# Softmax denominators from ones columns beside the values, divided between two 32x32 block transposes

## The chip, the core and the metric

One core of a Trainium2 chip runs the kernel. The metric is the device time of one execution in microseconds (us). Its engines work side by side and are tied by semaphores: TensorE (PE: matmuls, and PEld: the weight loads that go with them), VectorE (DVE), ScalarE (ACT), GpSimd (POOL), and SyncE (SP), which here only issues DMAs.

## The reference, cut to what matters

Input x is 8 images of 64 channels and 32x32 pixels, float32. The first layer is a window transformer block: layer norm over channels, windows of 8x8 = 64 tokens, 8 heads of depth 8, a relative position bias, softmax, projection and residual, a second layer norm, an MLP with gelu and its residual. The second layer is a gated convolution (a pointwise layer, a top-k mask over channels, depthwise 3x3, 5x5 and 7x7 kernels fused with a 1x1 layer). The part that the change touches:

```python
attn = einsum('bnhd,bmhd->bhnm', q * scale, k) + bias
attn = softmax(attn, axis=-1)                  # exp(a - max) / sum over the 64 keys
out = einsum('bhnm,bmhd->bnhd', attn, v).reshape(Bn, N, C)
return out @ w_proj + b_proj
```

## The kernel before, in words

**Layout.** Channels stand on the partitions, two images at once (partition 64*bh + channel), and the 4 x 1024 columns of pixels are cut in NG = 8 groups of G = 512 columns. One group holds NW = 8 windows (times two images). Each engine has its own program, written out by hand, and waits on counting semaphores; the order of the statements in each program is the order of its work.

**The attention phase** (38 to 201 us) is a software pipeline over the groups, `step(g, ...)`, once on each engine (PE L891, ACT L604, DVE L1236, POOL L456). Steps 0 and 1 stand alone, a hardware loop runs steps 2 and 3, then steps 4 to 7 stand alone. Step g of PE holds:
- `scores(g, w)` for w = 0 to 7 (L821): one matmul with the negative maxima (L832) and six with keys and queries split in a high and a low part (L835). ACT takes the exponentials of each window into `probs` (L581). `scores(g, 0)` waits for the maxima (`dv_minus`) and for the key blocks of this group (`k_blocks_in`); the instruction at which these waits are seen is L832.
- `values(g+1)` (L795), which ACT copies into `v_blocks` (`evacuate_v`, L576); `centered(g+2)` and `variance(g+2)` (helper line L763), the layer norm two groups ahead, with POOL making the low part of the squares (L286); `projection(g-1)` (L867), `centered2(g-1)` and `variance2(g-1)` for the second norm (L763 too).
- `weighted_values(g, 0)` and `sums(0)` after `scores(g, 4)`; then the passes over group g+1 that find the row maxima (`scores_for_max`, L813), woven between scores 5, 6 and 7, each reduced by DVE (`take_maximum`, L1189); `keys(g+2)` (L785, waits for maximum 5), `transpose_maxima(g+1)` (L819, waits for maximum 7), `queries(g+2)` (L790), and last `weighted_values(g, 1)` and `sums(1)`.

**The pieces that the change touches.** `weighted_values(g, quad)` (L839) multiplies the unnormalised probabilities of four windows with `v_blocks`: for each window p, each half of heads hh and each head j of the half one matmul of 32 stationary columns and 64 moving ones. In the 32 columns the values of a head fill two blocks of 8 (one for each image) and the rest is zero; hh = 1 accumulates onto hh = 0 in the same place of the PSUM bank PV, columns 0 to 255. `sums(quad)` (L853) runs the probabilities of the four windows against constant ones (L859) to get the denominators, laid out as the numerators are, in columns 256 to 511 of PV. On DVE, `divide_by_sums(g, quad)` (L1201) takes the reciprocal of those 256 columns (L1203) and multiplies (L1205) into `attended`. Quad 0 stands in DVE's step between maximum 2 and maximum 3 of the next group, quad 1 at the end of the step, behind `k_low` (L1179) and `q_low` (L1184). `weighted_values` waits for the `dv_att` of the quad before, because it writes PV again; `projection` waits for `dv_att` of both quads.

**The queue of SP.** In a fixed order, group by group: `spread_key_blocks(g+1)` (L385, four DMAs of 128 KB, after all scores of group g are done: `pe_scores`), `spread_queries(g+1, 1)` (L398, eight DMAs), `spread_keys(g+2)` (L371, eight DMAs), `spread_queries(g+2, 0)` (L398, eight).

**At the start** ACT loads its tables, sets all of `v_blocks` to zero in one operation (L522, waits for `eps_set`), and then waits for the first matmul. DVE copies the first constants (L1113) after the DMA `center_in`.

**After 201 us** come the MLP (L978, L990), the pointwise layer (L1002) and the gates, and from 247 us on the convolution (L1066), where PE is busy nearly throughout. The first of them are `mlp1(0)` and half of `mlp1(1)`, and then `projection(7)`.

## Time and profile before

| | us |
|---|---|
| runs | 345.48, 345.36, 343.74 (median 345.36) |
| the profiled execution, its own time | 343.12 |
| its span, first to last instruction | 341.3 |
| attention phase, first scores to last sums | some 163 of it |
| PE / DVE / ACT / POOL busy | 302.2 / 237.4 / 221.4 / 58.0 |
| TensorE's granted clock, mean | 0.98 of full speed; 1.00 from 38 us on up to the end of the attention |

The profiled execution takes 1.8 us more than its span, and was 0.6 to 2.4 us quicker than the three runs. Busy times of different engines overlap, so no one of them tells what a change is worth; the chain of waits and the timeline of a step do.

### The profile page before, as it was taken

The numbers are of one execution on the slowest core, as the hardware profiler recorded it, in microseconds if no ns is written. First come the engines' busy times: TensorE is split into PE (matmuls) and PEld (weight loads), VectorE is DVE, ScalarE is ACT, GpSimd is POOL, SyncE is SP. The second block draws the span as 40 slices with busy tenths as digits, with TensorE's granted clock in tenths as the row PEclk, the third lists the DMA queues.
The fourth block names the chain that finished last, engine by engine and source line by source line (L and its number), as shares of the span: only waits on it lengthen the run. The fifth ranks groups of instructions, "written<-read, shape, count | busy, mean of one in ns | idle before, by whom it ended". The sixth has DMA issues, their size and how long they took to land.

```text
span 341.3 us, 6607 instructions
## 1 busy us (share of the span) xinstructions
PE 302.2 (89%) x2570; PEld 215.9 (63%) x2570; DVE 237.4 (70%) x411; ACT 221.4 (65%) x371; POOL 58.0 (17%) x56
## 2 busy tenths in 40 slices
PE   2826888999999999999997999699899999999993
PEld 2514675767768776677675864354277777777772
DVE  2997148289496794976959635668999999976311
ACT  7693854867777677776673587986991673754500
POOL 4311001131331313313011160222220000000000
PEclk9987899999999999999999999999999999999999
DMA  7741154123141141411414000077003686777911
GB/s 170 152 92 53 51 144 84 48 50 80 50 83 48 40 95 47 80 48 41 94 52 89 17 2 0 1 162 160 0 3 70 131 181 133 147 139 154 189 32 31
DMA packets 31148, 27.67 MB, mean 81 GB/s; under 512 B 21008, under 2 KB 27664, under 8 KB 31120
## 3 DMA queue, kind: packets, MB, share of 16 engines
q1 hardware_dynamic: 30544, 26.48, 36.1%
q10 hardware_dynamic: 576, 0.79, 1.0%
q8 instruction: 20, 0.33, 0.5%
q14 instruction: 8, 0.07, 0.1%
HBM read 3.78 MB, written 2.10 MB: 17 GB/s over the span
## 4 chain that ended last, share of the span: by engine, by line
PE 58%; ACT 14%; DVE 13%; SPq 5%; DMA 4%; issue 3%; POOL 2%; DVEq 0%; ACTq 0%
PE psum L1066 25%; PE psum L835 5%; DVE maxima L1189 5%; PE psum L990 3%; PE psum L978 3%; PE psum L785 3%; PE psum L813 3%; PE psum L763 3%; ACT v_blocks L576 3%; DVE inv_sum L1203 2%; ACT q_blocks L566 2%; POOL parts L286 2%; ACT probs L581 2%; PE psum L850 2%; DMA probs<-in_raw 2%
## 5 line engine op out<-in xcount | busy, mean ns | idle before, releaser
L1066 PE MATMUL psum<-shifted,conv_w 128*128 128x512 f32 x336 | 86.6, 419 | 0.0
L1066 PEld LDWEIGHTS psum<-shifted,conv_w 128*128 128x128 f32 x336 | 63.9, 191 | 21.6 <-issue 1.3
L835 PEld LDWEIGHTS psum<-q_heads,k_blocks 128*128 128x128 f32 x384 | 54.6, 189 | 5.7 <-issue 1.9
L581 ACT ACTIVATE probs<-psum 128x512 f32<-128x512 f32 x64 | 38.1, 599 | 30.5 <-PE psum L835 30.3
L835 PE MATMUL psum<-q_heads,k_blocks 128*128 128x256 f32 x384 | 56.0, 281 | 0.0
L1189 DVE TENSOR_REDUCE maxima<-psum 128x8 f32<-128x512 f32 x64 | 40.3, 682 | 13.7 <-PE psum L813 12.7
L286 POOL TENSOR_TENSOR parts<-x,parts 128x256 fp32r<-128x256 f32 (+1 forms) x21 | 20.2, 975 | 84.0 <-ACT parts L589 51.1
L763 PE MATMUL psum<-parts,center_average 128*128 128x512 f32 x64 | 23.7, 454 | 11.9 <-DVE parts L286 6.8
L813 PE MATMUL psum<-k_heads,q_blocks 128*128 128x256 f32 x128 | 23.4, 306 | 12.1 <-DVE maxima L1189 5.0
L832 PE MATMUL psum<-minus_max,pick 128*128 128x512 f32 x64 | 30.1, 471 | 1.1 <-ACT probs L581 0.5
L813 PEld LDWEIGHTS psum<-k_heads,q_blocks 128*128 128x128 f32 x128 | 19.3, 201 | 17.7 <-DVE maxima L1189 6.1
L1203 DVE RECIPROCAL inv_sum<-psum 128x256 f32<-128x256 f32 x16 | 28.0, 1748 | 2.9 <-PE psum L859 2.8
L286 POOL TENSOR_TENSOR parts<-square_logvar,parts 128x512 fp32r<-128x512 f32 x14 | 18.2, 1301 | 68.5 <-ACT square_logvar L534 54.3
L272 ACT CAST conv_w<-conv_w 32x896 fp32r<-32x896 f32 x31 | 29.1, 938 | 0.4
L1433 DVE SCALAR_TENSOR_TENSOR x<-psum,weights,x 64x512 f32<-64x512 f32 x16 | 12.0, 748 | 21.0 <-PE psum L1066 20.9
L706 ACT CAST conv_w<-whole_w 128x896 fp32r<-128x896 f32 x8 | 7.5, 937 | 27.5 <-DVE whole_w L1408 18.8
L679 ACT ACTIVATE hidden<-psum,mlp_bias 128x512 f32<-128x512 f32 x32 | 19.6, 700 | 2.6 <-PE psum L978 2.6
L763 PEld LDWEIGHTS psum<-parts,center_average 128*128 128x128 f32 x64 | 10.3, 200 | 15.9 <-POOL parts L286 7.8
L566 ACT CAST q_blocks<-q_parts 32x512 fp32r<-32x512 f32 x32 | 19.7, 616 | 0.6
L978 PE MATMUL psum<-normed,mlp_w 128*128 128x512 f32 x64 | 18.1, 422 | 1.0 <-ACT hidden L679 1.0
L850 PEld LDWEIGHTS psum<-probs,v_blocks 128*32 128x32 f32 x1024 | 15.0, 110 | 6.2 <-issue 5.1
L492 POOL TENSOR_TENSOR images<-square_logvar,images 128x512 fp32r<-128x512 f32 x8 | 10.7, 1338 | 42.1 <-ACT images L689 42.1
(139 smaller groups left out, 463.8 us busy)
## 6 DMA issues: line engine op xcount, KB each, us to landing
shifted<-images SPq DMA_DIRECT2D x32, 332.5 KB, 5.5
k_blocks<-k_parts SPq DMA_DIRECT2D x32, 128.0 KB
q_heads<-q_parts SPq DMA_DIRECT2D x128, 32.0 KB, 1.8
k_heads<-k_parts SPq DMA_DIRECT2D x64, 32.0 KB, 1.8
out<-x SPq DMA_DIRECT2D x8, 256.0 KB, 4.7
x<-in_x SPq DMA_DIRECT2D x6, 256.0 KB, 4.9
x<-in_x SPq DMA_DIRECT2D x4, 128.0 KB, 4.3
weights<-in_weights ACTq DMA_DIRECT2D x1, 443.0 KB, 9.0
```

The costliest lines, as they stand in the source:

```text
L272: ins = copy(conv_w[bh][shift * KS:(shift + 1) * KS, part, :, C:], w[(shift - 1) * KS:shift * KS, :, 0:C])
L286: return engine.tensor_tensor(low, whole, high.bitcast(F32), ALU.subtract)
L566: ins = act.copy(q_blocks[r, half, :, bh * T:(bh + 1) * T].rearrange("p (s w) t -> p s w t", s=2), q_parts[r, par, :, 0, :].bitcast(F32).r ...
L581: act.activation(probs[:, w, :], psum[:, PROB0 + w % 2, :], ACT.Exp).then_inc(S["ac_probs"], 1)
L763: ins = pe.matmul(psum[:, bank, :], center_average[:, which, :], parts[:, part, :], start=part == 0, stop=part == 1)
L813: ins = pe.matmul(max_bank(w)[:, hh * G // 2:(hh + 1) * G // 2], q_blocks[:, hh, w, :], of_half(k_heads, hh)[:, :, w * T:(w + 1) * T], sta ...
L832: pe.matmul(bank, pick[:, w, :], minus_max[:, :, :], start=True, stop=False)
L835: ins = pe.matmul(bank[:, hh * G // 2:(hh + 1) * G // 2], k_blocks[:, hh, w // (NW // 2), k_part, w % (NW // 2), :], of_half(q_heads[:, q_ ...
L978: ins = pe.matmul(psum[:, HIDDEN0 + m, :], mlp1_w[:, part, f * 128:(f + 1) * 128], normed2[:, bh, bass.ds(n * G, G)], start=part == 0, sto ...
L1066: ins = pe.matmul(psum[:, CONV0 + bh, :], conv_w[bh][:, w_part, t, :], img[:, y:y + H - 1:2, x0:x0 + W], start=t == 0 and w_part + part == ...
L1189: dve.tensor_reduce(maxima[:, w * NH:(w + 1) * NH], max_bank(w).rearrange("p (h t) -> p h t", t=T), AX.X, ALU.max).then_inc(S["dv_max"], 1)
L1203: dve.reciprocal(inv_sum[:], psum[:, PV, 256:512]).then_inc(S["dv_inv"], 1)
```

## The change

The zeros beside the values become ones: a constant `sum_columns` (columns 16 to 31 are one where the row's image and the column's block agree) is copied over all of `v_blocks` at the start, after the first constants have landed. A value matmul then gives 16 rows of numerators and 16 of denominators for one half of heads; the two halves go side by side in PV instead of accumulating, so it still has 32 matmuls a quad, and `sums` is gone. Numerators and denominators then lie in different partitions, so DVE transposes the bank in blocks of 32x32 into `by_query`, takes the reciprocal of 32 numbers a partition, multiplies twice (128 numbers a partition each), and transposes the result back into `attended`. PE waits for the first transpose (`dv_turned`) before it writes PV again. Each of DVE's five instructions waits for the one that it reads from.

```diff
@@ -53,12 +53,11 @@
 
     "center": np.where(_bh[:, None] == _bh, (_p[:, None] == _p) - 1.0 / C, 0),
     "average": np.where(_bh[:, None] == _bh, 1.0 / C, 0),
+    "sum_columns": (np.arange(32) >= 16)[None] & (_bh[:, None] == np.arange(32) % 16 // HD),
     "ident": _p[:, None] == _p,
     "reverse": (_p % T)[:, None] == T - 1 - _p % T,
     "head_of_row": (_p % NH)[:, None] == np.arange(NH),
     "window_of_row": C * ((_p // NH % NW)[:, None] == np.arange(NW)),
-    "ones_by_head_half": (np.arange(64) // 32 == np.arange(64) % 32 // 16)[None]
-    & (_bh[:, None] == np.arange(64) % 16 // HD),
     "earlier": np.arange(C) < (_p % KS)[:, None],
     "valid": _valid(),
     "batch_of_row": _p[:, None] == np.arange(B),
@@ -90,7 +89,7 @@
 _RAT, NRAW = _columns(_RAW)
 
 
-NFIRST = _AT["average"][1]
+NFIRST = _AT["sum_columns"][1]
 
 
 def _constants():
@@ -171,8 +170,9 @@
         normed, rstd = (at(n, [128, G]) for n in ("normed", "rstd"))
         attended, rstd2 = (at(n, [128, G]) for n in ("attended", "rstd2"))
         projected = square2
-        inv_sum = at("inv_sum", [128, 4 * T])
+        inv_sum = at("inv_sum", [128, 2 * 4 * T // 32, 2])
         parts = at("parts", [128, 2, G], F32R)
+        by_query = at("by_query", [128, 2 * 4 * T // 32, 4, HD])
 
 
         normed2 = at("normed2", [128, 2, COLS], F32R)
...
@@ -518,9 +518,9 @@
 
             LN_AND_EXP, GELU = 6, 10
             load_tables(LN_AND_EXP)
-            act.wait_ge(S["eps_set"], 1)
-            act.activation(v_blocks[:].rearrange("p a b -> p (a b)"), eps[:, 0:1].to_broadcast([128, 2 * NW * NH * 32]), ACT.Copy, scale=0.0
-                           ).then_inc(S["v_zeroed"], 1)
+            act.wait_ge(S["center_in"], 16)
+            act.activation(v_blocks[:].rearrange("p a (b c) -> p (a b) c", c=32),
+                           const("sum_columns").unsqueeze(1).to_broadcast([128, 2 * NW * NH, 32]), ACT.Copy).then_inc(S["v_set"], 1)
 
             def high_of_x(n):
 
@@ -634,6 +634,7 @@
 
             square_of_centered(0)
             act.dma_start(weights[:, _WAT["vec"][1]:], d["weights"][:, _WAT["vec"][1]:]).then_inc(S["weights_in"], 16)
+            act.wait_ge(S["eps_set"], 1)
             act.wait_ge(S["consts_in"], 16)
             for half in range(2):
                 ins = act.activation(k_blocks[:, half, :, 0], reversal().rearrange("p (s w) t -> p s w t", s=2), ACT.Copy, scale=not_in_half(half))
@@ -645,7 +646,7 @@
             evacuate_k(0, 0)
             evacuate_q(0, 0)
             block_queries(1, 0)
-            act.wait_ge(S["v_zeroed"], 1)
+            act.wait_ge(S["v_set"], 1)
             evacuate_v(0, 0)
             square_of_centered(1)
             late = range(NW // 2, NW)
@@ -841,23 +842,15 @@
                 pe.wait_ge(S["ac_v"], 4 * (g + 1))
                 pe.wait_ge(S["ac_probs"], NW * g + 4 * quad + 4)
                 if not (isinstance(g, int) and g == 0 and quad == 0):
-                    pe.wait_ge(S["dv_att"], 2 * g + quad)
+                    pe.wait_ge(S["dv_turned"], 2 * g + quad)
                 for p in range(4):
                     for hh in range(2):
                         for j in range(4):
                             w, head = 4 * quad + p, 4 * hh + j
-                            at = (w * NH + head) * 32 - 16 * hh
-                            pe.matmul(psum[32 * j:32 * j + 32, PV, p * T:(p + 1) * T], v_blocks[:, par, at:at + 32],
-                                      probs[:, w, head * T:(head + 1) * T], start=hh == 0, stop=hh == 1)
-
-            def sums(quad):
-
-                for hh in range(2):
-                    for j in range(4):
-                        head = 4 * hh + j
-                        a = _AT["ones_by_head_half"][0] + 32 * hh
-                        ins = pe.matmul(psum[32 * j:32 * j + 32, PV, 256:512], consts[:, a:a + 32],
-                                        probs[:, 4 * quad:4 * quad + 4, head * T:(head + 1) * T], start=hh == 0, stop=hh == 1)
+                            at = (w * NH + head) * 32
+                            column = (hh * 4 + p) * T
+                            ins = pe.matmul(psum[32 * j:32 * j + 32, PV, column:column + T], v_blocks[:, par, at:at + 32],
+                                            probs[:, w, head * T:(head + 1) * T], start=True, stop=True)
                 ins.then_inc(S["pe_pv"], 1)
 
             def projection(c):
@@ -908,7 +901,6 @@
                     variance(far)
                 scores(g, 4)
                 weighted_values(g, 0, par)
-                sums(0)
                 maximum_pass(0, 1)
                 scores(g, 5)
                 maximum_pass(2, 3)
@@ -927,7 +919,6 @@
                 if far is not None:
                     queries(far)
                 weighted_values(g, 1, par)
-                sums(1)
 
             pe.wait_ge(S["dv_center"], 1)
             centered(0)
@@ -1110,7 +1101,7 @@
 
             dve.memset(eps[:], EPS1).then_inc(S["eps_set"], 1)
             dve.wait_ge(S["center_in"], 16)
-            dve.tensor_copy(center_average[:].rearrange("p m c -> p (m c)"), consts[:, 0:NFIRST]).then_inc(S["dv_center"], 1)
+            dve.tensor_copy(center_average[:].rearrange("p m c -> p (m c)"), consts[:, 0:_AT["average"][1]]).then_inc(S["dv_center"], 1)
             dve.wait_ge(S["x_first"], 32)
             for s in range(2):
                 ins = dve.tensor_copy(stripe(parts[:, 0, :], s), x_view(0, s))
@@ -1199,11 +1190,24 @@
                                   const("head_of_row").unsqueeze(2).to_broadcast([128, NH, T]), ALU.mult).then_inc(S["dv_minus"], 1)
 
             def divide_by_sums(g, quad):
-                dve.wait_ge(S["pe_pv"], 2 * g + quad + 1)
-                dve.reciprocal(inv_sum[:], psum[:, PV, 256:512]).then_inc(S["dv_inv"], 1)
-                dve.wait_ge(S["dv_inv"], 2 * g + quad + 1)
-                dve.tensor_tensor(attended[:, quad * 4 * T:(quad + 1) * 4 * T], psum[:, PV, 0:4 * T], inv_sum[:],
-                                  ALU.mult).then_inc(S["dv_att"], 1)
+
+                n = 2 * g + quad + 1
+                dve.wait_ge(S["pe_pv"], n)
+                if not (isinstance(n, int) and n == 1):
+                    dve.wait_ge(S["dv_att"], n - 1)
+                dve.transpose(by_query[:].rearrange("p n k d -> p (n k d)"), psum[:, PV, :]).then_inc(S["dv_turned"], 1)
+                dve.wait_ge(S["dv_turned"], n)
+                dve.reciprocal(inv_sum[:], by_query[:, :, 2:4, 0]).then_inc(S["dv_inv"], 1)
+                dve.wait_ge(S["dv_inv"], n)
+                blocks = 4 * T // 32
+                for hh in range(2):
+                    mine = slice(hh * blocks, (hh + 1) * blocks)
+                    ins = dve.tensor_tensor(by_query[:, 0:blocks, 2 * hh:2 * hh + 2, :], by_query[:, mine, 0:2, :],
+                                            inv_sum[:, mine, :].unsqueeze(3).to_broadcast([128, blocks, 2, HD]), ALU.mult)
+                ins.then_inc(S["dv_ratios"], 1)
+                dve.wait_ge(S["dv_ratios"], n)
+                dve.transpose(attended[:, quad * 4 * T:(quad + 1) * 4 * T], by_query[:, 0:blocks].rearrange("p n k d -> p (n k d)")
+                              ).then_inc(S["dv_att"], 1)
 
             def add_residual(c):
                 dve.wait_ge(S["ac_proj"], c + 1)
```

## Rows read from the trace of the kernel before

**Rows 1.** The page, part 4: the chain that ended last, by engine.

```profile
PE 58%; ACT 14%; DVE 13%; SPq 5%; DMA 4%; issue 3%; POOL 2%; DVEq 0%; ACTq 0%
```

**Rows 2.** The chain in order of time, step 3 into step 4: start us, us, what.

```profile
115.24 1.67 DVE inv_sum L1203
116.94 0.42 DVE attended L1205
...
119.30 1.10 PE psum L785 x2
...
121.89 1.03 PE psum L850 x64
122.92 0.86 PE psum L859 x16
123.79 0.43 PE psum L832
...
137.01 1.67 DVE inv_sum L1203
```

**Rows 3.** Groups by line and form: busy us, mean ns of one | idle before.

```profile
L1203 DVE RECIPROCAL inv_sum<-psum 128x256 f32<-128x256 f32 x16 | 28.0, 1748 | 2.9 <-PE psum L859 2.8
L859 PE MATMUL psum<-probs,consts 128*32 128x256 f32 x256 | 16.7, 379 | 0.0
```

**Rows 4.** The same view: the nearest rows to DVE's new operations.

```profile
L1189 DVE TENSOR_REDUCE maxima<-psum 128x8 f32<-128x512 f32 x64 | 40.3, 682 | 13.7 <-PE psum L813 12.7
L1211 DVE TENSOR_TENSOR x<-square_logvar,x 128x256 f32<-128x256 f32 x16 | 6.1, 422 | 14.1 <-ACT square_logvar L585 14.1
L1370 DVE TENSOR_TENSOR gate_memory<-gate_memory 128x128 f32<-128x128 f32 x2 | 0.6, 291 | 0.1
```

**Rows 5.** Timeline, SP's key blocks and PE's first scores after them, steps 0 and 3.

```profile
51.84 2.72 SPq L385 DMA_DIRECT2D k_blocks<-k_parts  x4
58.41 0.50 PE L832 MATMUL psum<-minus_max,pick 128*128 128x512 f32 x1
...
117.73 2.74 SPq L385 DMA_DIRECT2D k_blocks<-k_parts  x4
```

**Rows 6.** The chain in order of time, end of step 5 to step 7.

```profile
174.20 1.79 DMA k_heads<-k_parts
...
181.12 0.61 SPq L385
...
183.13 3.39 DMA k_blocks<-k_parts
...
186.76 0.47 PE psum L832
```

**Rows 7.** Timeline, POOL and DVE reading SBUF: steps 3 and 5.

```profile
116.54 1.29 POOL L286 TENSOR_TENSOR parts<-square_logvar,parts 128x512 fp32r<-128x512 f32 x1 [1.99 <-ACT square_logvar L594]
120.67 1.41 POOL L286 TENSOR_TENSOR parts<-x,parts 128x256 fp32r<-128x256 f32 x2 [2.84 <-ACT parts L528]
121.36 1.26 DVE L1198 TENSOR_TENSOR minus_max<-maxima_t,consts 128x512 fp32r<-128x512 f32 x1
...
164.90 0.69 DVE L1198 TENSOR_TENSOR minus_max<-maxima_t,consts 128x512 fp32r<-128x512 f32 x1
```

**Rows 8.** Timeline, step 7 and behind it: start us, us, what [idle before].

```profile
193.82 1.28 POOL L286 TENSOR_TENSOR parts<-x,parts 128x512 fp32r<-128x512 f32 x1 [12.61 <-ACT parts L589]
195.48 0.64 PE L763 MATMUL psum<-parts,center_average 128*128 128x512 f32 x2
...
203.22 0.42 DVE L1205 TENSOR_TENSOR attended<-psum,inv_sum 128x256 f32<-128x256 f32 x1
...
204.13 1.02 PE L867 MATMUL psum<-attended,weights 128*128 128x512 f32 x2
```

**Rows 9.** Timeline, the start: first constants copied, `v_blocks` zeroed.

```profile
2.99 0.29 DVE L1113 CAST center_average<-consts 128x256 fp32r<-128x256 f32 x1 [2.11 <-DMA consts<-in_consts]
3.44 3.62 ACT L522 ACTIVATE v_blocks<-eps 128x4096 f32<-128x4096 f32 x1
```

More of the change, by code:

```diff
@@ L227, in conv_seq_kernel @@
         S = {n: sem(n) for n in (
-            "zeroed", "k_blocks_zeroed", "k_blocks_set", "q_blocks_set", "k_heads_set", "q_heads_set0", "q_heads_set1", "v_zeroed", "eps_set", "center_in", "consts_in", "x_first", "x_in0", "x_in1", "x_in2", "x_in3", "qkv_in", "raw_in", "weights_in", "rel_in0", "rel_in1",
+            "zeroed", "k_blocks_zeroed", "k_blocks_set", "q_blocks_set", "k_heads_set", "q_heads_set0", "q_heads_set1", "v_set", "eps_set", "center_in", "consts_in", "x_first", "x_in0", "x_in1", "x_in2", "x_in3", "qkv_in", "raw_in", "weights_in", "rel_in0", "rel_in1",
             "pe_qkv_bias", "dv_qkv_bias", "qkv_ready", "pe_biases", "weights_ready", "dv_rel_flipped", "dv_rel_high", "dv_rel_low", "dv_center", "dv_scaled", "dv_high",
@@ L232, in conv_seq_kernel @@
             "ac_sq", "ac_log", "ac_rstd", "ac_q_high", "ac_k_high", "ac_v", "ac_probs", "ac_proj", "ac_sq2", "ac_log2", "ac_rstd2",
-            "dv_normed", "dv_k_low", "dv_q_low", "k_heads_in", "q_blocked", "k_blocks_in", "q_heads_in0", "q_heads_in1", "dv_max", "dv_maxt", "dv_minus", "dv_inv", "dv_att", "dv_x1", "dv_normed2",
+            "dv_normed", "dv_k_low", "dv_q_low", "k_heads_in", "q_blocked", "k_blocks_in", "q_heads_in0", "q_heads_in1", "dv_max", "dv_maxt", "dv_minus", "dv_turned", "dv_inv", "dv_ratios", "dv_att", "dv_x1", "dv_normed2",
             "pe_mlp1", "pe_mlp2", "pe_pw1", "ac_gelu", "ac_relu", "dv_x2", "dv_hsum",
```

## The prediction

> **What bounds the kernel now.** I read the page's chain first: PE holds over half of what ends the kernel, ACT and DVE some 14% each [rows 1]. Busy times don't price the change, because the attention phase is a loop over engines. So I followed the chain in order of time through one step [rows 2]. The reader is to see there that the divide of quad 0 (L1203, L1205) and the sums of quad 1 (L859) are both links: DVE divides, takes the next maxima, PE makes keys, queries, weighted values, sums, and only then the first scores of the next group (L832). From reciprocal to reciprocal it is 137.01 - 115.24 = 21.77 us. Everything that is taken out of this loop counts once a step, unless a second path into L832 is nearly as late. That path exists: SP's key blocks [rows 5, 6].
>
> **Part 1, PE.** The 32 value matmuls of a quad stay as they are (64 instructions, 1.03 us); that the second half of heads starts afresh instead of accumulating changes no shape, and I take it at nothing, with no cover needed [rows 2]. The 16 instructions of the sums go (256 in 16 quads), 0.86 us in the chain at quad 1 [rows 2, 3]. At quad 0 the PE then waits for ACT's query blocks anyway, so there they free only idle time, except in step 7, where no next group follows.
>
> **Part 2, DVE.** Before: 1.67 + 0.02 + 0.42 = 2.12 us, from 115.24 to 117.36 [rows 2]. The reciprocal costs 1748 ns for 256 numbers; an addition of 128 costs 291 and one of 256 costs 422, so 131 for 128 more and about 160 ns fixed [rows 3, 4]. The reciprocal thus takes (1748 - 160)/256 = 6.2 ns a number, and 32 numbers 0.36 us. The two multiplications are 0.29 each, with 0.08 of overlap: 0.50. No transpose stands in the trace. The nearest row for the one out of PSUM is the maximum, which reads 128x512 there, one number after another: 0.68; for the one inside SBUF the 128x256 addition, 0.42 [rows 4]. Three hand-overs with a wait add 0.02 each, as between reciprocal and product before: 0.06. Sum 0.68 + 0.36 + 0.50 + 0.42 + 0.06 = 2.02, less the 0.08 by which the first overlaps the maximum before it: 1.94, against 2.12. So DVE gains 0.18 a divide. Bounds of the unknown: nothing in the rows reads PSUM faster than one number at a time, so no gain beyond this is likely (0.1 at most, if the SBUF one ran as quickly as the cheapest copies); at half that pace (2.04 ns a number beside the 160 fixed) the transposes would be 1.20 and 0.68, together 0.78 more. I take the near end, since maximum and addition both lie there.
>
> The Trainium skill ("Vector Engine (DVE) Microarchitecture Reference", section 3.8) says that the 32x32 array sustains one element per cycle per lane when it transposes. No row here shows it; by it the two transposes would cost what I took.
>
> **Part 3, waits and queues.** DVE's new waits are for its own work, priced above, and `dv_att` of the quad before is long done. PE's wait for `dv_turned` comes about 1.5 us earlier than that for `dv_att`, and was not felt. Behind the divide on DVE stand the maxima 3 to 7, for which keys and the transposed maxima wait; this is the chain above.
>
> **What is late next.** SP issues the four key-block DMAs when the last scores of a group are done. In step 6 nothing else is in the way: issue from 181.12, the last one from 183.13, landed 3.39 later at 186.52, L832 at 186.76: 5.64 us from the first issue to L832 [rows 6]. In step 3 SP begins at 117.73, so the key blocks let L832 start at 123.37, and the chain has it at 123.79 [rows 2, 5]. Only 0.42 us of the 0.86 + 0.18 can be had there. In step 0 SP begins at 51.84, so 57.48 against 58.41: up to 0.9.
>
> **The sum.** Step 0 into 1: 0.9. Steps 1 to 4 into the next: 4 x 0.42 = 1.7. Step 5 into 6: nothing, for there SP's queue of key blocks, queries and keys is the chain; its last DMA (174.20 + 1.79) releases the next pass on PE. Step 6 into 7: nothing, key blocks again [rows 6]. Step 7: the sums of quad 0 stood before `centered2`, but that one waits for POOL, ready at 193.82 + 1.28 = 195.10 against a start of 195.48, and the PE starts slower out of a wait: 0.3 us gained; the sums of quad 1 give 0.86. `projection(7)`, at 204.13, would then come at 203.0, but needs the last divide, done at 203.64 before; 0.3 earlier by its start and 0.18 by its length it is done at about 203.15. So 0.95 for step 7 [rows 8]. From there to the end PE work shifts as a whole. At the start ACT's copy costs what the zeroing did (the same 4096 numbers, 3.62 us); its new wait is for a DMA that DVE had at 2.99 us, and ACT began only at 3.44, behind its table load, so a DMA of 288 columns for 256 is covered [rows 9]. Total 0.9 + 1.7 + 0.95 = 3.55 us.
>
> The profiled execution took 343.12, so 339.6 of its kind. The median of the runs is 2.2 us above it. On the median's footing I forecast **341.8 us**.
>
> **Rivals.**
>
> *A. The divide meets POOL.* When POOL reads SBUF, a DVE operation with two SBUF inputs stands still: L1198 takes 1.26 beside POOL's pair of 0.7 us each and 0.69 alone [rows 7]. The old divide read PSUM. The new multiplications read SBUF twice. The first would start 1.08 us after the divide's start (115.24, less the overlap of 0.08), at 116.24, the second at 116.45; POOL's low part of the squares starts at 116.54 and runs 1.29. DVE is first by 0.09 us, less than my error on the transpose. If it is second, the multiplication ends about 0.15 after POOL's 117.83, and the divide at 118.42, 1.06 later than before; less 0.86, each of the four full steps loses 0.2 instead of gaining 0.42. Steps 0 and 7 have no such meeting. Total -0.9 + 0.8 - 0.95 = -1.05: 344.3 on the median's footing.
>
> The Trainium skill ("SBUF — State Buffer", "Who interferes with whom") speaks against the change here: a DVE operation with two SBUF inputs and a GpSimd operation that reads SBUF exclude each other for the whole instruction, and the first to issue goes first. The trace agrees in L1198.
>
> *B. The key blocks don't bind.* If their 5.64 us is shorter in full steps than in step 6, the four steps give 1.04 each: 0.9 + 4.2 + 0.95 = 6.05, so 339.3. For it: landing times scatter. Against it: the same four DMAs with the same queries behind them.
>
> *C. Slower: transposes at half pace.* They cost 0.78 more, and both multiplications now start after POOL's operation (116.76 against 116.54). They wait for 117.83, end at 118.19, and the second transpose at 118.89: 1.53 later than before, 0.67 net of the sums, in four steps 2.7. Step 0 still gains 0.2 and step 7 nothing, as `projection(7)` waits for the divide. Slower by 2.5: 347.9. It decides from a divide of some 3.0 us on, where the 0.86 of the sums is eaten up. For it: the operation is nowhere in the trace; against it: no DVE row of one PSUM input runs at such a pace.
>
> *D. The key blocks bind harder.* If they take 0.3 us longer in full steps than in step 6, those give 0.1 each and the total is 0.9 + 0.4 + 0.95 = 2.25: 343.1.
>
> **How the numbers follow.** Forecast 0.42, A 0.2, B 0.13, C 0.12, D 0.08, and 0.05 for trouble I don't see (slower). What a measurement here can tell from no change is about 0.5%, 1.7 us. Faster: forecast, B, D and a little of A: 0.64. Same: most of A, and edges of the others: 0.21. Slower: C and the rest: 0.15. The range goes from B with half a microsecond to spare, 338.5, to 346.0, which takes in A with an unlucky start; only C and some of the tails are left out.
>
> **What would show it.** The transpose of the bank near 0.7 us, the reciprocal near 0.36, the whole divide near 2.0; no L859; PE waiting for a key-block DMA ahead of L832 in the full steps, the time from reciprocal to transpose of the next step 21.35 us; steps 5 and 6 unchanged from L832 to L832. The forecast is wrong if the multiplications show 1.2 us instead of 0.29 (A), if PE never waits for key blocks (B), or if the transposes take over 1 us (C).

## The result and the profile after

| | before | after |
|---|---|---|
| median of the runs, us | 344.84 (343.69 to 345.48, 13 runs) | 347.12 (344.71 to 350.80, 13 runs) |
| ratio | | 1.0071 [1.0041, 1.0102] |
| the profiled execution, us | 343.12 | 349.57 |
| its span, us | 341.3 | 347.7 |
| mean granted clock of TensorE in it | 0.983 | 0.960 |

The change makes the kernel 0.7% slower. The ratios here and below leave out executions that lie more than 1.5% above the fastest of the same kernel (two of after's 13, five of the 12 of `before_drop_q1`, one each of `after_lock_pad48` and `after_lock_pad64`). I had forecast 341.8 us, faster by 1.0%, and a range up to 346.0. The profiled execution of after is one of the longer ones of its kind, 2.45 us above its median, so the 6.4 us between the two spans show in large what is 2.3 us between the medians. The runs of after also scatter over 6.1 us, those of before over 1.8.

What the change touches came out almost as worked out. The groups by line and form, of after (busy us, mean ns of one | idle before):

```profile
L1198 DVE STREAM_TRANSPOSE by_query<-psum 128x512 f32<-128x512 f32 x16 | 11.3, 704 | 1.5 <-PE psum L852 1.5
L1205 DVE TENSOR_TENSOR by_query<-by_query,inv_sum 128x128 f32<-128x128 f32 x32 | 8.0, 291 | 0.6
L1209 DVE STREAM_TRANSPOSE attended<-by_query 128x256 f32<-128x256 f32 x16 | 7.1, 446 | 0.6
L1200 DVE RECIPROCAL inv_sum<-by_query 128x32 f32<-128x32 f32 x16 | 5.7, 353 | 0.6
```

On PE the 16.7 us of sums are gone. On DVE the 28.0 us of reciprocals [rows 3] and 16 products of 0.42 us are gone, and 32.1 us stand in their place. (`minus_max` is L1189 now, the key scores L833 and L836, the maximum pass L814, `mlp1` L969.)

So the loss is somewhere else. The chain in order of time, steps 5 to 7 of after, answers to [rows 6]:

```profile
174.91 3.73 DMA k_heads<-k_parts
...
178.78 0.71 PE psum L814 x4
...
185.31 0.61 SPq L385
...
187.32 3.40 DMA k_blocks<-k_parts
...
190.96 0.76 PE psum L833
191.73 1.28 PE psum L836 x6
```

The last k_heads DMA took 3.73 us where it took 1.79 before. And the six matmuls of L836, which take 0.71 to 0.73 us in the chain elsewhere, took 1.28. Timeline of PE, behind the first of its three longest waits of the attention phase, and behind the last:

```profile
69.55 0.71 PE L814 MATMUL psum<-k_heads,q_blocks 128*128 128x256 f32 x4 [2.04 <-DMA k_heads<-k_parts]
70.10 0.40 PE L833 MATMUL psum<-minus_max,pick 128*128 128x512 f32 x1
70.33 1.34 PE L836 MATMUL psum<-q_heads,k_blocks 128*128 128x256 f32 x6
...
193.23 1.48 PE L836 MATMUL psum<-q_heads,k_blocks 128*128 128x256 f32 x6
```

Stretches of both kernels, first after, then before (us, busy time with instructions of PE, PEld, DVE, ACT, POOL, then PEclk, DMA share, GB/s):

```profile
66.00:70.40 4.40, 2.36 (x75) 2.05 (x74) 1.03 (x2) 3.22 (x6) 1.01 (x1) 1.00 0.17 52
70.50:73.90 3.40, 3.40 (x15) 3.11 (x15) 2.54 (x6) 1.08 (x2) 0.18 (x1) 0.50 0.12 40
176.00:179.60 3.60, 0.96 (x18) 0.81 (x7) 0.31 (x1) 1.61 (x3) 1.26 (x1) 1.00 0.16 50
179.70:183.10 3.40, 3.40 (x16) 3.11 (x15) 2.55 (x5) 1.05 (x2) 0.00 (x0) 0.50 0.12 39
185.00:190.00 5.00, 2.81 (x75) 2.11 (x73) 4.12 (x9) 1.92 (x3) 0.10 (x1) 1.00 0.56 113
190.00:196.80 6.80, 5.84 (x22) 5.33 (x23) 3.74 (x9) 1.54 (x3) 0.00 (x0) 0.50 0.11 35
```

```profile
66.00:70.40 4.40, 4.04 (x97) 3.21 (x96) 1.51 (x3) 3.54 (x6) 0.69 (x1) 1.00 0.16 45
70.50:73.90 3.40, 3.40 (x26) 3.16 (x25) 3.23 (x5) 2.17 (x4) 1.41 (x2) 1.00 0.16 43
190.00:196.80 6.80, 6.80 (x112) 5.44 (x111) 3.64 (x6) 3.99 (x8) 1.28 (x1) 1.00 0.01 2
```

A granted clock of 0.50 is the 1.2 GHz level. After falls to it three times in the attention phase: twice about 1 us behind the end of a wait of PE for a DMA (2.04 and 2.64 us), and once within such a wait (2.01 us). Before never does between 38 us and the end of that phase. In the first of these stretches PE gets through 15 matmul instructions where before has 26.

The first scores of each group tell where the time went. Their distance from SP's first key-block issue is the second row of each pair:

| group | 1 | 2 | 3 | 4 | 5 | 6 | 7 | `mlp1` | end |
|---|---|---|---|---|---|---|---|---|---|
| before, us | 58.41 | 80.18 | 101.95 | 123.72 | 145.48 | 167.26 | 186.76 | 201.23 | 341.3 |
| from SP's issue | 6.57 | 5.99 | 5.99 | 5.99 | 5.99 | 6.00 | 5.64 | | |
| after, us | 58.12 | 81.73 | 103.16 | 124.59 | 146.00 | 168.41 | 190.96 | 206.95 | 347.7 |
| from SP's issue | 5.65 | 5.65 | 5.69 | 5.70 | 5.67 | 6.68 | 5.65 | | |

The steps from group 2 to 5 are 21.43, 21.43 and 21.41 us long, against 21.77: 0.34 gained in each. Step 1 loses 1.84 (k_heads late, then the low clock), step 5 loses 0.63 (key blocks 1.0 late), step 6 loses 3.05 (k_heads late, low clock), step 7 loses 1.52 (low clock), and from `mlp1` to the end 0.7 are lost. So the main question is why transfers that the change doesn't touch land late in some steps and not in others.

### The profile page after: what moved, and what is told of

Read it like the earlier page. It is cut to its first block, busy times and chain, and to the rows that moved or that the text cites. A ratio compares the mean times of both kernels' runs of the same rounds, so it can differ in the third digit from the quotient of the medians.

```text
span 347.7 us, 6159 instructions
## 1 busy us (share of the span) xinstructions
PE 295.7 (85%) x2314; PEld 216.0 (62%) x2314; DVE 234.2 (67%) x459; ACT 221.6 (64%) x371; POOL 60.3 (17%) x56
## 4 chain that ended last, share of the span: by engine, by line
PE 54%; ACT 13%; SPq 11%; DMA 9%; DVE 6%; issue 3%; POOL 2%; DVEq 0%; ACTq 0%
PE psum L1057 25%; PE psum L836 7%; DMA k_blocks<-k_parts 5%; SPq L385 4%; PE psum L814 4%; PE psum L764 3%; PE psum L981 3%; SPq L398 3%; PE psum L833 3%; PE psum L969 3%; SPq L371 2%; DMA probs<-in_raw 2%; POOL parts L286 2%; ACT v_blocks L576 2%; ACT probs L581 2%
## 5 line engine op out<-in xcount | busy, mean ns | idle before, releaser
L836 PEld LDWEIGHTS psum<-q_heads,k_blocks 128*128 128x128 f32 x384 | 57.8, 200 | 5.8 <-issue 1.7
L836 PE MATMUL psum<-q_heads,k_blocks 128*128 128x256 f32 x384 | 58.9, 292 | 0.0
L814 PE MATMUL psum<-k_heads,q_blocks 128*128 128x256 f32 x128 | 24.4, 317 | 18.6 <-DMA k_heads<-k_parts 7.9
L286 POOL TENSOR_TENSOR parts<-x,parts 128x256 fp32r<-128x256 f32 (+1 forms) x21 | 21.8, 1050 | 87.4 <-ACT parts L589 54.5
L833 PE MATMUL psum<-minus_max,pick 128*128 128x512 f32 x64 | 30.9, 482 | 6.8 <-DMA k_blocks<-k_parts 6.2
L764 PE MATMUL psum<-parts,center_average 128*128 128x512 f32 x64 | 24.8, 473 | 13.2 <-DVE parts L286 7.7
L814 PEld LDWEIGHTS psum<-k_heads,q_blocks 128*128 128x128 f32 x128 | 20.4, 215 | 21.9 <-ACT q_blocks L566 9.1
L764 PEld LDWEIGHTS psum<-parts,center_average 128*128 128x128 f32 x64 | 11.1, 214 | 17.2 <-POOL parts L286 8.0
L833 PEld LDWEIGHTS psum<-minus_max,pick 128*128 128x128 f32 x64 | 12.8, 200 | 11.4 <-issue 9.1
L1215 DVE TENSOR_TENSOR x<-square_logvar,x 128x256 f32<-128x256 f32 x16 | 6.1, 422 | 20.4 <-ACT square_logvar L585 20.4
L969 PE MATMUL psum<-normed,mlp_w 128*128 128x512 f32 x64 | 18.5, 425 | 1.4 <-ACT hidden L680 1.4
```

What stands on the lines that cost most here:

```text
L286: return engine.tensor_tensor(low, whole, high.bitcast(F32), ALU.subtract)
L764: ins = pe.matmul(psum[:, bank, :], center_average[:, which, :], parts[:, part, :], start=part == 0, stop=part == 1)
L814: ins = pe.matmul(max_bank(w)[:, hh * G // 2:(hh + 1) * G // 2], q_blocks[:, hh, w, :], of_half(k_heads, hh)[:, :, w * T:(w + 1) * T], sta ...
L833: pe.matmul(bank, pick[:, w, :], minus_max[:, :, :], start=True, stop=False)
L836: ins = pe.matmul(bank[:, hh * G // 2:(hh + 1) * G // 2], k_blocks[:, hh, w // (NW // 2), k_part, w % (NW // 2), :], of_half(q_heads[:, q_ ...
L969: ins = pe.matmul(psum[:, HIDDEN0 + m, :], mlp1_w[:, part, f * 128:(f + 1) * 128], normed2[:, bh, bass.ds(n * G, G)], start=part == 0, sto ...
```

## The experiments

Eleven kernels ran, in four lots, each timed in five rounds beside the kernel before. Whether key blocks were late is read from the distance from SP's first key block to the first scores.

**Lot 1: the missing sums.** The first suspicion was the missing PE work. `ballast_both` and `ballast_q0` give it back to after, its results unused:

```diff
+            def ballast(quad):
+                for hh in range(2):
+                    for j in range(4):
+                        head = 4 * hh + j
+                        pe.matmul(psum[32 * j:32 * j + 32, MAX0 + quad, 256:512], const("sum_columns"),
+                                  probs[:, 4 * quad:4 * quad + 4, head * T:(head + 1) * T], start=True, stop=True)
...
                 weighted_values(g, 0, par)
+                ballast(0)
```

(`ballast_both` has `ballast(1)` behind the second `weighted_values` too.) `before_drop_q0` and `before_drop_q1` take the work out of before from step 1 on, with DVE's divide as it was (it then divides by stale denominators):

```diff
-            def sums(quad):
+            def sums(quad, g):
+                if quad in DROPPED and not (isinstance(g, int) and g == 0):
+                    return
```

> The changed kernel plus matmuls of the shape of the old sums (8 a quad, results thrown away) behind the value matmuls of both quads; the output is unchanged. TensorE gets back its old work, DVE keeps the new divide. Theory 1 (TensorE, idle where the sums used to stand, falls to its low clock in stretches): the clock is back to 0.98 as before the change, no fall between 60 and 205 us, and the time is that of the kernel before or a little below, 343.5 to 345. Rival 2 (the new DVE divide with its transposes costs the time): slower still than the changed kernel, 348 to 350. Rival 3 (SP's DMAs merely land later by chance): about as spread as the changed kernel, 345 to 350.

> The changed kernel plus such matmuls behind the value matmuls of quad 0 alone, where TensorE waits for ScalarE's query blocks anyway. Theory 1 (low clock out of idle time): they cost nothing by themselves and keep the clock up, so the gain of quad 1 shows: 341.5 to 343.5, clock 0.98, and the step is 21.4 us long. Rival 2 (DVE's divide): as the changed kernel or slower, 347 to 349. Rival 3 (DMAs by chance): as spread as the changed kernel.

> The kernel before with the sums of quad 0 left out from step 1 on (the denominators there are stale); DVE as before. By the chain of waits these sums hide behind ScalarE's query blocks, so by the chain alone this is 0 to 0.5 us faster. Theory 1: taking away work that nobody waited for makes it slower, 346 to 348, with clock falls like the changed kernel's around 70, 180 or 190 us. Rival 2 (DVE's divide is to blame): no slower than before, 344 to 345.

> The kernel before with the sums of quad 1 left out from step 1 on (stale denominators), where they stand in the chain. By the chain: 4 steps by 0.42 us and 0.86 at the end, 342 to 343. Theory 1: with quad 0's sums kept the clock mostly holds, so 342 to 344. If the idle time ahead of the first scores (the wait for the key blocks) is what lowers the clock: slower than before, 345 to 348.

Measured: `ballast_both` 346.56 us, ratio 1.0030 [1.0003, 1.0058]; `ballast_q0` 350.29, 1.0146 [1.0113, 1.0180]; `before_drop_q0` 350.10, 1.0148 [1.0103, 1.0192]; `before_drop_q1` 349.94, 1.0084 [1.0040, 1.0128]. Giving half of the work back is worse than none, and taking half of it from before costs as much as the whole change does or more, with the old divide in place. So the loss doesn't need the new divide. Theory 1, the low clock, met none of the four times that it gave. Low clock alone doesn't explain them either: over its runs `ballast_q0` has the mean clock of after (0.967 both), and is 3 us slower. What the three slower kernels share is late key blocks, three steps in a row: 6.79, 6.93, 6.86 us in `ballast_q0`, 6.99, 6.81, 6.85 in `before_drop_q0`, in `before_drop_q1` 7.03, 6.90, 6.80 one step further on.

The DMA view of such a step names what is new in it. Before, from SP's first key block to the first scores (95.96 to 101.95), in 40 slices, and its queues (packets, MB, share of 16 engines):

```profile
GB/s 0 0 0 0 0 0 0 0 53 162 125 130 149 137 130 152 142 137 132 118 111 180 246 263 229 190 190 190 164 151 212 29 116 103 0 0 48 158 14 0
...
q1 hardware_dynamic: 2256, 0.62, 58.3%
```

`before_drop_q0`, the same step (98.12 to 104.93):

```profile
GB/s 0 0 0 0 0 0 0 54 164 116 140 143 134 157 146 138 134 98 141 245 260 239 190 182 153 242 199 63 72 109 0 3 8 9 12 12 0 6 175 12
...
q1 hardware_dynamic: 2256, 0.62, 52.3%
q8 instruction: 1, 0.02, 1.0%
```

The same 2256 packets and 0.62 MB. But there is one packet more, on the queue "instruction", and the data end in a trickle of 3 to 12 GB/s over a microsecond: nearly all of the transfer has landed and a small rest is late. After's late step 5 to 6 (161.73 to 168.41) has both:

```profile
GB/s 0 0 0 0 0 0 0 31 153 136 133 147 135 146 147 133 130 110 123 206 256 248 222 219 288 150 173 97 67 117 5 8 9 11 11 18 31 160 6 0
...
q8 instruction: 1, 0.02, 0.9%
```

Whose instructions these are follows from their number. The pages of before, after and of `after_lock_pad64` (below), part 1 and the queue in part 3:

```profile
PE 302.2 (89%) x2570; PEld 215.9 (63%) x2570; DVE 237.4 (70%) x411; ACT 221.4 (65%) x371; POOL 58.0 (17%) x56
...
q8 instruction: 20, 0.33, 0.5%
```

```profile
PE 295.7 (85%) x2314; PEld 216.0 (62%) x2314; DVE 234.2 (67%) x459; ACT 221.6 (64%) x371; POOL 60.3 (17%) x56
...
q8 instruction: 18, 0.29, 0.3%
```

```profile
PE 295.4 (86%) x2698; PEld 216.2 (63%) x2698; DVE 235.7 (69%) x459; ACT 221.5 (65%) x371; POOL 60.3 (18%) x56
...
q8 instruction: 21, 0.34, 0.4%
```

5140, 4628 and 5396 matmuls and weight loads by 20, 18 and 21 pieces: 257 each time, whatever DVE has. (Over all 13 kernels, where such a quotient depends on how the last piece falls, it is 254 to 266.) A piece is 16 KB and takes 0.9 to 1.5 us. So this is TensorE's own program, loaded while it runs. (The Trainium skill, "Runtime: NRT & Kernel Launch", "Instruction fetch mechanics", has the same size: program memory is refilled in blocks of 16 KiB, 256 instructions, by a DMA queue of the sequencer. It calls the cost mostly hidden. For the engine itself nothing here speaks against that; what the runs below show is a cost to the transfers beside it.) A step of before has two quads of sums, 64 such instructions, more than one of after: 512 with them, which is two pieces, 448 without. In before the pieces therefore come at nearly the same place in every step (94.4 and 103.8 us, 115.0 and 126.8, 136.7 and 147.2: ahead of SP's key blocks, and behind the first scores). In after they drift through the step, and sooner or later one meets k_heads (67.2, 176.6 us) or the key blocks (165.9 us). I call this theory F and tested it by moving the pieces alone.

**Lot 2.** `before_pad32` and `after_pad40` put one-column matmuls, once, where PE waits for the first keys; `after_lock` puts 8 of them where each quad's sums were, so that a step has 512 instructions again:

```diff
+            def filler(count):
+                for m in range(count):
+                    j = m % 4
+                    pe.matmul(psum[32 * j:32 * j + 32, MAX0, 256 + m:257 + m], consts[:, 32 * j:32 * j + 32], vec[:, 1:2],
+                              start=True, stop=True)
...
             centered(1)
+            filler(32)
```

```diff
+            def filler(quad):
+                for m in range(8):
+                    j = m % 4
+                    pe.matmul(psum[32 * j:32 * j + 32, MAX0 + quad, 256 + m:257 + m], const("sum_columns"),
+                              probs[:, 4 * quad, m:m + 1], start=True, stop=True)
```

> The kernel before with 32 matmuls of one column each (results unused, 4 TensorE instructions each, 128 in all) put once, ahead of step 0, where TensorE waits 4.59 us for the keys by head; nothing else is touched. Theory F (instruction fetches): TensorE's program comes in pieces of 16 KB, one for about 256 of its instructions, by DMAs on the queue called instruction; a piece that comes while the last 128 KB of key blocks lands delays that landing. 128 instructions more move every later piece half a period forward, from about 94 and 104 us to about 89 and 100.5, 122.4, 144.0, 165.7 us, which is 4.5 us after SP issues the key blocks, where steps of other kernels ran late. So the first scores of steps 2 to 6 come 6.8 us after SP's first key-block issue instead of 5.99, with a wait for the key-block DMA, and the kernel takes 348 to 350 us. Theory D (the divide) and theory C (too little work on TensorE lowers its clock): the steps' work is the same, so 5.99 us in each step and no change of the time within 0.5%.

> The kernel after with 40 such one-column matmuls (160 TensorE instructions) at the same place. Theory F: the pieces that came at 67.2 us (k_heads of step 1) and at 165.9 and 176.6 us (key blocks and k_heads of step 6) move to about 61.7, 154.9 and 172.2 us, all harmless; others move in: about 122.9 and 144.8 us, 4.0 and 4.5 us after SP's key blocks of steps 4 and 5 (counting the first scores they precede), and 133.0 us at k_heads of step 4. So lateness (6.7 us and more from SP's first key block to the first scores) leaves steps 6 and 1 and appears before the first scores of groups 4 and 5. The total moves by up to 3 us either way, likeliest 345 to 347. Theories D and C: the late places stay at steps 1 and 6 and the time stays at 347.

> The kernel after with 8 one-column matmuls (32 TensorE instructions) where each quad's sums were, in every step: the count of TensorE instructions in a step is the one of before again, and with it the places of the pieces (about 94.5 and 104 us and so on, as in before), with hardly any of the work. Theory F: steps 21.4 to 21.5 us long with 5.65 us from SP's key blocks to the first scores everywhere and none late, about 342 to 343 us, faster than both kernels. Theory C: nearly no work was given back, so the low-clock stretches of after stay and the time is 346 to 347. Theory D: 347, nothing of the divide is changed.

Measured: `before_pad32` 345.94 us, ratio 1.0023 [1.0000, 1.0046], a miss. The pieces didn't go where I had reckoned; they came at 103.1 and 124.2 us, at the first scores (103.12, 124.90), and no step was late (5.99). It says nothing against F, but theories C and D had told this time and these distances. And I can't place a piece from the count alone. `after_pad40`: 344.33, 0.9983 [0.9956, 1.0011], 2.8 us below after's median (timed in another lot) with the same work in every step. Step 1 is 21.40 us long and the key blocks of step 5 to 6 are on time (5.64 us), as F had it. The lateness that F told for groups 4 and 5 didn't come (5.81 and 6.20 us), although in group 4 a piece came 4.79 us behind SP's issue, and the time is below the likeliest 345 to 347. In step 6 PE still waits 1.90 us for k_heads, though these are on time: PE starts 1.92 us behind SP's last k_heads issue, as in before. `after_lock`: 343.72, 0.9959 [0.9931, 0.9987], 0.7 above the 342 to 343 that F gave, but below both kernels and below what theories C and D gave (346 to 347). Its distances are 5.71, 5.68, 5.66, 5.65, 5.65, 5.65 and 5.86.

**Lots 3 and 4: onto the key blocks on purpose.** The same filler with 48 and with 64 matmuls, in before and in `after_lock`.

> The kernel before with 48 one-column matmuls instead of 32 at the same place, 64 TensorE instructions more than before_pad32. In before_pad32 a piece of TensorE's program came just at the first scores of a step (103.1 us, first scores 103.12 us) and no step was late. Theory F: 64 instructions more bring it about 1.2 us forward, 4.8 us after SP's first key block, where a piece delayed the last key blocks in one step of before_drop_q1 (4.75 us) and hardly in one of after_pad40 (4.8 us): some steps late by about 1 us (6.0 to 7.0 us from SP's first key block to the first scores, with a key-block wait), 346 to 350 us in all. Theories C and D: 5.99 us in each step and the time of before_pad32, 345.9, plus 0.3 us for the longer start.

> The kernel before with 64 one-column matmuls at the same place, 128 TensorE instructions more than before_pad32. Theory F: the piece comes 1.6 to 1.8 us ahead of the first scores, 4.2 to 4.4 us after SP's first key block, the place at which all late steps so far had theirs: steps 2 to 6 late by 0.8 to 1.0 us each (6.8 to 7.0 us), 349 to 351 us in all. Theories C and D: 5.99 us in each step and at most 1 us over before_pad32 for the longer start, 347.

> after_lock with the 48 one-column matmuls ahead of step 0 of before_pad48. Theory F: with as many TensorE instructions ahead of each step as before_pad48, the pieces of its program come at the same places of the steps, 4.1 to 4.8 us after SP's first key block, and the last key blocks land late: 6.7 to 7.0 us to the first scores in most of the steps 1 to 5, where after_lock takes 5.65, so about 5 us more than after_lock, 348 to 349 us. Theories C and D: 343.7 plus 0.3 us, 344.

> after_lock with 64 one-column matmuls ahead of step 0, as before_pad64, whose pieces came 2 us ahead of SP's key blocks and 3 us behind the first scores and where no step was late. Theory F: steps of 21.4 us with 5.65 us from SP's key blocks to the first scores, the time of after_lock within 0.5%: 343 to 345 us, below the kernel before. If it is as late as after_lock_pad48, the fillers themselves cost the time and theory F falls.

| kernel | median us | ratio | from SP's issue to first scores, groups 2 to 6 | pieces between SP's issue and the first scores |
|---|---|---|---|---|
| `before_pad48` | 349.46 | 1.0132 [1.0089, 1.0176] | 6.97 6.73 7.04 6.71 6.93 | 4.49 4.15 4.73 3.53 4.12 |
| `before_pad64` | 345.58 | 1.0013 [0.9996, 1.0030] | 5.99 5.99 5.98 5.99 5.99 | none |
| `after_lock_pad48` | 352.64 | 1.0141 [1.0086, 1.0196] | 6.64 7.16 6.74 6.92 6.95 | 4.16 4.92 4.14 4.15 4.21 |
| `after_lock_pad64` | 343.40 | 0.9942 [0.9915, 0.9969] | 5.68 5.68 5.70 5.66 5.68 | none |

(For `after_lock_pad48` the medians differ by 2.2%, the ratio by 1.4%: its executions are two near 349, three near 352.7 and one at 355.66 us, so the size is uncertain.) `before_pad48` and `before_pad64` differ from each other and from before by matmuls of one column ahead of step 0, and every full step of the one is 0.7 to 1.05 us late. F had told some late steps in `before_pad48` and 346 to 350 us, which came, and every step late in `before_pad64` and 349 to 351 us, which didn't: again the place missed while the effect is there. Then `after_lock_pad48` and `_pad64`, told by analogy, had the steps that were told. The time of `_pad64` came as told as well, that of `_pad48` is 3.6 us above the 348 to 349. Timeline, SP's key blocks and the first scores of group 3, `before_pad64` and then `before_pad48`:

```profile
96.32 2.71 SPq L385 DMA_DIRECT2D k_blocks<-k_parts  x4
...
102.31 0.50 PE L832 MATMUL psum<-minus_max,pick 128*128 128x512 f32 x1
```

```profile
97.89 2.71 SPq L385 DMA_DIRECT2D k_blocks<-k_parts  x4
...
104.62 0.47 PE L832 MATMUL psum<-minus_max,pick 128*128 128x512 f32 x1 [0.68 <-DMA k_blocks<-k_parts]
```

Over all 13 kernels, groups 2 to 6 (65 cases): a piece starts 3.5 to 4.95 us behind SP's issue in 23 of them; 20 of these are late (6.6 to 7.2 us), 3 are not (5.65, 5.73, 5.81). Of the 42 others none is late; the highest has 6.20 us and no wait for a DMA. (The bound of 4.95 is where the cases put it: one at 4.99 was on time.) Groups 1 and 7 are less clean: of 12 cases with a piece in that span only three are late (in group 1 6.89 us in `before_drop_q1`, where 6.57 is usual without the change, and 6.53 in `ballast_q0`, with a wait of 0.87 for the key blocks; in group 7 7.31 in `before_pad48`). So a piece in this place can delay the key blocks, and need not.

The packets show how. The four key-block DMAs are 2048 packets of 256 bytes. In the 45 steps of groups 2 to 6 that were on time, all have started by 4.86 us behind SP's issue. In 19 of the 20 late ones, 1 to 48 of them start later, and the last of them at 5.59 to 6.09 us, when the piece has ended or just as it ends. In the step of `before_drop_q0` above the piece runs from 4.35 to 5.42 us, and 13 packets follow from 5.41 us on. So all but a few packets pass the piece, and most of those few start only at its end. (The one exception, group 4 of `before_pad48`, is late without such packets. In groups 1 and 7 the three late cases have them, and no other has.)

The k_heads of step 6 behave alike. Where no piece starts within 2 us behind SP's last k_heads issue, PE starts the maximum pass 1.91 or 1.92 us behind it in six of seven kernels (in `after_lock_pad48` 3.54, with another wait, for ACT's query blocks). In the six where one starts 0.4 to 1.7 us behind it (after is one of them), it is 2.94 to 3.87 us.

## Why the prediction was wrong

*"The 16 instructions of the sums go."* Right in work: 0.86 us out of the chain at quad 1. Not counted was that they are also 32 entries of TensorE's program a quad. That is the step that failed. I took the landing times as fixed (the key blocks' 5.64 us, "steps 5 and 6 unchanged", the k_heads DMA's 1.79), while they hold only as long as no piece of program falls among them. In step 5, which I called unchanged, the key blocks came 1.0 us late, and in step 6, the other one, k_heads 1.9 late.

*The clock.* I priced every PE row at the full clock because the profile had it at 1.00 from 38 us on. A late DMA makes PE wait 2 us, and behind such waits the clock stood at half for 3.4 to 6.8 us. At `after_pad40`'s full clock step 7 is 13.36 us long, in after 15.99: 2.6 us there alone. And the wait needn't be a collision's: in `after_pad40` k_heads were on time, PE waited 1.90 us for them at 176.16 us because it had less work ahead of them, and from 176.8 to 180.2 us the clock stood at half. That the waits bring the low clock is what the rows suggest by their order. I didn't test it by itself, and it isn't strict: in `before_drop_q1` a wait of 1.83 us for key blocks was followed by it and in `after_lock_pad48` one of 1.76, but in `ballast_q0` waits of 1.70, 1.81 and 1.76 us weren't.

*"What is late next", 4 x 0.42.* Right, the key blocks bind: PE waits 0.56 to 0.60 us for them in the undisturbed steps, and SP's issue to first scores is 5.65 to 5.70 against 5.64. The gain was 0.34 a step. Most of the 0.08 that is missing is a slip of reading: the chain's row has L832 at 123.79, but the matmul started at 123.72, which is the 5.99 us of the table. Rivals B and D didn't occur.

*DVE's divide, 1.94 against 2.12.* Each operation is within 0.03 us of its estimate, but the gain is half of the forecast. Timeline of DVE, one divide in step 3 of after:

```profile
114.27 2.10 DVE L1180 TENSOR_REDUCE maxima<-psum 128x8 f32<-128x512 f32 x3 [1.62 <-PE psum L814]
116.29 0.70 DVE L1198 STREAM_TRANSPOSE by_query<-psum 128x512 f32<-128x512 f32 x1
117.03 0.35 DVE L1200 RECIPROCAL inv_sum<-by_query 128x32 f32<-128x32 f32 x1
117.42 0.49 DVE L1205 TENSOR_TENSOR by_query<-by_query,inv_sum 128x128 f32<-128x128 f32 x2
117.95 0.45 DVE L1209 STREAM_TRANSPOSE attended<-by_query 128x256 f32<-128x256 f32 x1
118.32 3.10 DVE L1180 TENSOR_REDUCE maxima<-psum 128x8 f32<-128x512 f32 x5
```

Counted as the forecast did, from the end of the maximum before it (116.37) to its own end (118.40), it is 2.03 against 2.12: the hand-overs cost 0.04 each instead of 0.02, and the gain is 0.09 instead of 0.18. Of the two fresh costs, the transpose from PSUM at 704 ns for 512 numbers clears rival C (half pace). The 446 ns for 256 numbers lie 258 ns below it, 1.0 ns a number, as the additions have (131 ns for 128). The Trainium skill's one element per cycle per lane ("Vector Engine (DVE) Microarchitecture Reference", section 3.8) agrees with that in kind; the length of a cycle isn't in the trace.

*Rival A, POOL.* DVE was first, by more than the 0.09 forecast: L1205 starts at 117.42, POOL's part of the squares at 117.69 and takes 1.37 us instead of 1.29 [rows 7]. POOL isn't waited for there. The Trainium skill's rule ("SBUF — State Buffer", "Who interferes with whom") is that such operations exclude each other and the first to issue goes first. The order fits it. The size is less clear: DVE's second multiplication runs to 117.91, and POOL's operation is only 0.08 us longer.

*Step 7, 0.95, "From there to the end PE work shifts as a whole".* Half right. Step 7 of `after_pad40`, without low clock, is 13.36 against 14.47 us, so 1.11 shorter. But behind it PE meets ACT. `after_pad40`, PE and then before, PE (timeline):

```profile
201.75 2.14 PE L976 MATMUL psum<-normed,mlp_w 128*128 128x512 f32 x8
204.32 1.22 PE L976 MATMUL psum<-normed,mlp_w 128*128 128x512 f32 x4 [0.43 <-ACT hidden L680]
```

```profile
201.23 3.06 PE L978 MATMUL psum<-normed,mlp_w 128*128 128x512 f32 x12
```

`mlp1` stops after two blocks for ACT's first GELU, which stands behind ACT's table load. From the start of `mlp1` to the end it is 140.77 us instead of 140.05: 0.7 of the 1.1 goes back. This happens in every kernel without the full sums of quad 1 (140.67 to 140.79) and in none with them (140.03 to 140.09).

*The sum.* With the key blocks on time in every step the change is worth 0.5% in the medians (`after_lock_pad64`, 343.40 against 345.05), not 1.0%. Its profiled span, 341.5 us, is that of before, 341.3, which was a quick execution of its kind, so the profiles can only show the terms, not the 1.65 us. Against before, by the first scores, with the forecast in brackets: start to group 0 +1.5 us (0), step 0 -0.6 (-0.9), steps 1 to 4 -1.3 (-1.7), steps 5 and 6 together +0.1 (0), step 7 -0.1 (-0.95), `mlp1` to the end +0.6 (0).

The start isn't the clock's: PE's first matmul stands at 6.93 us instead of 5.73, behind DVE's first copy of x, which waits for a DMA until 5.49 instead of 4.30, and SP's first key block at 22.29 instead of 20.85. So nearly all of the 1.5 is there before the clock falls at 22.5 us. Over the seven kernels with the change the first matmul starts at 6.55 to 7.10 us, over the six without it at 5.72 to 7.00, so it isn't shown that the change causes this.

In step 7 the 16 fillers take some 0.4 us, and PE stands still for 0.70 us ahead of its fifth scores (192.04 us). The profile puts that down to ACT's `probs`, but the probabilities that L833 waits for were done by 190.2 us. What it also needs are the second half's queries, and their last packet ends 10.2 us behind SP's first key block, where `after_lock` and `after_pad40` have 8.9; a piece runs from 189.32 to 190.73 us. So even this kernel has one meeting left, by these rows. Beside the collisions, then, the terms that were mis-sized are the 0.42 (it was 0.33 on average), step 0 and the last step with what follows it. With the collisions, the change is worth -0.7%.

**What stays open.** The trace doesn't show on which of the 16 DMA engines a packet runs. That a piece sits ahead of data packets on one of them would fit the few packets that start only at its end, and the cases in which a piece did no harm, but the engine itself wasn't seen. How much of the 0.7% is late data and how much the low clock behind it wasn't separated. Where a piece comes couldn't be told from the instruction count: in `before_pad64`, told to have them 4.2 to 4.4 us behind SP's issue, none came between it and the first scores. Only profiled executions show their pieces. That the placements repeat from run to run is inferred from the times: `before_pad48`, 347.82 to 352.72, lies wholly above `before_pad64`, 343.94 to 346.09. And key blocks aren't all that can come last: in group 7 of `ballast_both` 7.95 us passed without a piece in the harmful span, but there PE waited for nothing ahead of the first scores; its own work, in a stretch of low clock, was what took the time.

## What to carry to other kernels

TensorE's program is DMA traffic, so adding or taking away matmuls moves loads that compete with the kernel's small, latency-bound transfers. When a change that shortens the chain makes the kernel slower or the scatter larger, compare the landing times of untouched DMAs and look at the instruction queue before blaming the new code. A few one-column matmuls at a place where PE waits move these loads, and they are worth a trial by themselves: between 48 and 64 of them the ratio moved from 1.0132 to 1.0013 in before and from 1.0141 to 0.9942 in `after_lock`, more than the change itself. And where a loop's step is a whole number of pieces long, its pieces stay where they are, good or bad; in a step that isn't they drift, and may meet one of the harmful places.

## What the runs showed of the hardware

- TensorE's instructions come in pieces of 16 KB, one for 257 matmuls and weight loads (20, 18, 21 pieces; 254 to 266 over all kernels), each taking 0.9 to 1.5 us beside the data. One that starts 3.5 to 4.95 us behind SP's issue, while the last key blocks land, delayed them by about 1 us in 20 of 23 cases of groups 2 to 6, and in 3 of 12 of groups 1 and 7.
- Such a piece holds up a few packets and not the transfer: in 19 of the 20 late steps 1 to 48 of the 2048 packets of 256 bytes started later than in any step on time.
- 16 one-column matmuls more, ahead of a loop of which nothing was changed, moved the whole kernel by 3.9 us (345.58 with 64 of them, 349.46 with 48).
- A 32x32-block transpose of 128x512 fp32 numbers from PSUM takes 704 ns, of 128x256 within SBUF 446 ns; a reciprocal of 32 numbers a partition 353 ns, of 256 it was 1748.
- One-column matmuls are cheap: 8 behind each quad left the full steps at 21.4 us.
